# Attention scores in matmuls of 64 rows over six PSUM banks, with the softmax steps in a new order

## The reference

```python
q = split_heads(x @ w_q)
k, v = split_heads(text @ w_k), split_heads(text @ w_v)             # 56 keys
k_ip, v_ip = split_heads(ip_h @ w_k_ip), split_heads(ip_h @ w_v_ip) # 8 keys
out  = merge(softmax(q @ k.T / sqrt(32)) @ v)
out += merge(softmax(q @ k_ip.T / sqrt(32) + mask_ip) @ v_ip)
return out @ w_out + b_out + x
```

## Time and profile before

| | us |
|---|---|
| median of 3 runs | 879.96 (879.78 to 881.93) |
| the profiled execution | 879.29 |
| its span | 877.5 |
| TensorE busy | 872.8 (99%) |
| TensorE weight loads busy | 750.8 (86%) |
| VectorE busy | 724.0 (83%) |
| ScalarE busy | 589.9 (67%) |
| GpSimd busy | 524.2 (60%) |

### The profile page before, as it was taken

The page is one execution under the profiler, slowest core; times in us unless marked ns, Lnnn a source line. Parts: engine busy times, 40 slices in busy tenths (PEclk is TensorE's granted clock), DMA queues, the critical chain, the costliest instruction groups (busy, mean ns, idle before and its releaser), DMA issues.

```text
span 877.5 us, 13695 instructions
## 1 busy us (share of the span) xinstructions
PE 872.8 (99%) x4716; PEld 750.8 (86%) x4716; DVE 724.0 (83%) x1018; ACT 589.9 (67%) x986; POOL 524.2 (60%) x421
## 2 busy tenths in 40 slices
PE   9999999999999999999999999999999999999998
PEld 8899888888888888888888888888888888888877
DVE  7779889797888879697887879787897979888785
ACT  7766685857767585766768486675758577574773
POOL 1059776492846648293755739384664929466581
PEclk9999999999999999999999999999999999999999
DMA  9924223021030303003030301203030210301011
GB/s 324 356 95 135 83 77 127 1 67 70 1 127 1 135 1 116 12 8 128 1 128 1 135 1 41 87 1 135 1 127 1 85 50 1 120 25 37 1 49 72
DMA packets 34225, 64.99 MB, mean 74 GB/s; under 512 B 4480, under 2 KB 6784, under 8 KB 34048
## 3 DMA queue, kind: packets, MB, share of 16 engines
q1 hardware_dynamic: 33888, 62.84, 21.2%
q10 hardware_dynamic: 288, 1.44, 0.4%
HBM read 40.34 MB, written 23.59 MB: 73 GB/s over the span
## 4 chain that ended last, share of the span: by engine, by line
PE 96%; DVE 2%; POOL 1%; ACT 1%; DMA 0%; issue 0%; SPq 0%
PE bank L95 25%; PE bank L97 25%; PE bank L96 25%; PE bank L1155 8%; PE bank L1175 4%; PE bank L1176 4%; PE bank L1064 1%; PE bank L1067 1%; PE bank L1070 1%; DVE total L225 1%; PE bank L1085 1%; PE bank L1082 1%; DMA w_raw<-in_L_xattn_w_k 0%; DVE top L219 0%; POOL prob L178 0%; PE bank L1107 0%
## 5 line engine op out<-in xcount | busy, mean ns | idle before, releaser
L517 POOL TENSOR_TENSOR oT_lo<-o_raw,oT_hi 128x512 fp32r<-128x512 f32 x78 | 100.9, 1294 | 225.0 <-ACT oT_hi L693 225.0
L178 POOL TENSOR_TENSOR prob<-prob,top 128x1120 f32<-128x1120 f32 x126 | 177.5, 1439 | 0.0
L184 POOL TENSOR_TENSOR prob<-prob,inv 128x1120 f32<-128x1120 f32 x126 | 177.2, 1439 | 0.0
L95 PE MATMUL bank<-xT_hi,wq_hi 128*128 128x512 f32 x400 | 163.0, 407 | 0.0
L937 DVE TENSOR_TENSOR o_raw<-bank,pv_part 64x512 f32<-64x512 f32 x160 | 110.2, 689 | 62.4 <-ACT pv_part L689 59.9
L95 PE MATMUL bank<-oT_hi,wo_hi 128*128 128x512 f32 (+1 forms) x405 | 157.4, 389 | 0.0
L96 PE MATMUL bank<-oT_lo,wo_hi 128*128 128x512 f32 (+1 forms) x405 | 156.7, 387 | 0.0
L97 PE MATMUL bank<-oT_hi,wo_lo 128*128 128x512 f32 (+1 forms) x405 | 156.6, 387 | 0.0
L97 PE MATMUL bank<-xT_hi,wq_lo 128*128 128x512 f32 x400 | 156.5, 391 | 0.0
L96 PE MATMUL bank<-xT_lo,wq_hi 128*128 128x512 f32 x400 | 155.8, 389 | 0.0
L689 ACT ACTIVATE pv_part<-bank 64x512 f32<-64x512 f32 x160 | 94.7, 592 | 62.5 <-PE bank L1176 59.9
(11 more groups left out here) (124 smaller groups left out, 1694.3 us busy)
## 6 DMA issues: line engine op xcount, KB each, us to landing
xin<-in_xT SPq DMA_DIRECT2D x16, 1280.0 KB, 6.9
outT<-res SPq DMA_DIRECT2D x79, 256.0 KB, 6.7
w_raw<-in_L_xattn_w_k SPq DMA_DIRECT2D x8, 320.0 KB, 4.9
w_raw<-in_L_xattn_w_k_ip SPq DMA_DIRECT2D x8, 320.0 KB, 5.4
w_raw<-in_L_xattn_w_v_ip SPq DMA_DIRECT2D x8, 320.0 KB, 3.4
w_raw<-in_L_xattn_w_v SPq DMA_DIRECT2D x8, 320.0 KB, 3.3
v_raw<-v_scratch SPq DMA_DIRECT2D x14, 140.0 KB
prob<-in_textT SPq DMA_DIRECT2D x8, 224.0 KB, 4.4
```

Of the source, the lines that this page charges most:

```text
L95: nc.tensor.matmul(dst, a_hi, b_hi, start=first, stop=False)
L178: ins = eng.tensor_tensor(s, s, top[:, t, n, :].unsqueeze(2).broadcast_to([P, HEADS, k1 - k0]), ALU.subtract)
L184: ins = eng.tensor_tensor(s, s, inv[:, t, n, :].unsqueeze(2).broadcast_to([P, HEADS, k1 - k0]), ALU.mult)
L517: nc.gpsimd.tensor_tensor(oT_lo[:, m, :], o_raw[:, m % 2, :], oT_hi[:, m, :].bitcast(F32), ALU.subtract).then_inc(oT_lo_done, 1)
```

## The change

**Scores.** The key parts move into one tensor `k_parts`, in which each half of 64 rows has its own 2 heads x 64 keys = 128 columns. A step becomes six matmuls of 64 rows and 128 columns, the upper and the lower half in turn, each half into a bank of its own (`score_units`). Four steps fill two banks, and the banks rotate over 0 to 5; banks 4 and 5 are those of the value products, so the third pair of banks waits for `pv_added`. The copy now scatters a bank over `prob` (`score_dst`).

```diff
-        def units_for_tile(t):
-            return -(-(t + 1) * SW // 512)
+        def units_for_tile(t):
+            return 2 * -(-(t + 1) * KD // RUN)
...
+        def score_units(pe, g, u, b, new_batch):
+            if u == 0:
+                wait(pe, score_copied, UNITS * g)
+            elif u == 1:
+                wait(pe, pT_lo_done, PAIRS * g)
+            elif u == 2:
+                wait(pe, pv_added, PAIRS * g)
+            else:
+                pe.wait_ge(score_copied, UNITS * g + 2 * u - 4)
...
+            for i in (1, 0, *range(2, RUN)) if u == 1 else range(RUN):
...
+                for n, (q, part) in enumerate(((qT_hi, 0), (qT_hi, 1), (qT_lo, 0))):
+                    for r in range(2):
+                        rows = slice(r * HP, (r + 1) * HP)
+                        ins = nc.tensor.matmul(s_bank[(2 * u + r) % 6][:, i * PW:(i + 1) * PW], q[rows, m, q_cols], k_parts[rows, m, part, :], start=n == 0, stop=n == 2)
```

```diff
         def maxima(dve, g, t):
-            dve.wait_ge(mask_added, GT * g + t + 1)
+            dve.wait_ge(score_copied, UNITS * g + units_for_tile(t))
             for n, (k0, k1) in enumerate(SPANS):
+                if n == 1:
+                    dve.wait_ge(mask_added, GT * g + t + 1)
...
+                    oT_part(g - 1, KD - 1)
+                    for t in range(GT - 1):
+                        maxima(dve, g, t)
+                    split_x(0, 2)
+                    output(g - 1, 1 - u, 0)
+                    maxima(dve, g, GT - 1)
+                    split_x(2, 3)
+                    output(g - 1, 1 - u, 1)
+                    sums(dve, g, 0)
+                    output(g - 1, 1 - u, 2)
+                    split_x(3, 4)
+                    sums(dve, g, 1)
+                    split_x(4, 5)
+                    output(g - 1, 1 - u, 3)
+                    sums(dve, g, 2)
+                    sums(dve, g, 3)
+                    output(g - 1, 1 - u, 4)
+                    if u == 0:
+                        v_lo_part(b)
```

**TensorE at the start of `values`.** The eight transposes of pairs 0 and 1 go tile by tile, both pairs for a tile, where before they went pair by pair:

```diff
-                    p_transpose(g, 0)
-                    p_transpose(g, 1)
+                    pe.wait_ge(score_copied, UNITS * (g + 1))
+                    for t in range(GT):
+                        pe.wait_ge(prob_done, GT * g + t + 1)
+                        for p in range(2):
+                            ins = transpose_tile(g, p, t)
```

```diff
-                sp.dma_start(ctx_raw[:, 0, 0:TT], textT[0:P, :]).then_inc(ctx0_loaded, 16)
                 load_chunk(0)
+                sp.dma_start(ctx_raw[:, 0, 0:TT], textT[0:P, :]).then_inc(ctx0_loaded, 16)
...
+                    if name == "q":
+                        sp.dma_start(xin[:, 0, k, :], x_half[0, 0][:, k, :]).then_inc(first_x_loaded[k], 16)
...
+                nc.gpsimd.memset(v_parts[:].rearrange("p n s c -> p (n s c)").bitcast(F32), 0.0).then_inc(v_zeroed, 1)
+                normalise(pool, 0, 3, 1)
```

More of the change, by code:

```diff
@@ L486, in _ @@
                                         pattern=[[-1, P]], channel_multiplier=1).then_inc(ident_made, 1)
[L487 to L488 removed]
+                nc.gpsimd.memset(k_parts[:].rearrange("p m s c -> p (m s c)").bitcast(F32), 0.0).then_inc(k_zeroed, 1)
                 mine = pool_chunks
@@ L979, in last_softmax @@
                 def last_softmax(g):
-                    for t in range(GT - 1):
+                    oT_part(g - 1, KD - 1)
+                    for t in range(GT):
                         maxima(dve, g, t)
                     sums(dve, g, 0)
-                    maxima(dve, g, GT - 1)
-                    sums(dve, g, 1)
                     dve.wait_ge(max_done, GT * (g + 1))
                     subtract_top(nc.vector, GT - 1).then_inc(last_max_subbed, 1)
-                    for t in range(2, GT):
+                    for t in range(1, GT):
                         sums(dve, g, t)
@@ L1027, in values @@
                                 pT_part(g, p)
+                        if keys is not None and s in (0, 2):
+                            k_lo_part(dve, keys, range(s, s + 2))
                 def group(g, u, b):
                     softmax(g, u, b)
-                    values(g)
-                nc.vector.memset(v_parts[:, :, 1, :].bitcast(F32), 0.0).then_inc(v_lo_zeroed, 1)
+                    values(g, keys=b + 1 if u == 1 else None)
+                v_lo_part(0)
                 q_lo_part(dve, 1, 1)
@@ L1036, in _ @@
                 group(1, 1, 0)
-                with dve.Fori(1, B - 1) as b:
+                for b in range(1, B - 1):
                     group(2 * b, 0, b)
@@ L1137, in _ @@
                         ins.then_inc(k_ipT_ready, 1)
-                for n in range(UNITS):
-                    score_unit(pe, 0, n, 0, True)
+                for u in range(UNITS // 2):
+                    score_units(pe, 0, u, 0, True)
                 for k in range(KC):
@@ L1216, in scores @@
                 def scores(g, b, new_batch):
-                    for n in range(UNITS):
-                        score_unit(pe, g, n, b, new_batch)
+                    for u in range(UNITS // 2):
+                        score_units(pe, g, u, b, new_batch)
                     for m in range(KD):
@@ L1239, in last_group @@
                 def last_group(g, b):
-                    for n in range(UNITS):
-                        score_unit(pe, g, n, b, False)
+                    for u in range(UNITS // 2):
+                        score_units(pe, g, u, b, False)
                     for m in range(KD - 1):
```

164 lines of the change are left out of this document (75 added, 89 removed).

## The result

The changed kernel takes 905.53 us (median of 4 runs, 905.46 to 905.88), the kernel before 879.94 in the same comparison (879.78 to 881.93): ratio 1.0286, 95% interval 1.0268 to 1.0304. The profiled execution took 905.46 us, its span is 903.7 for 877.5. The forecast of 849.6 us is wrong in sign, and the time lies far outside the range of 838 to 877.

What follows compares the result with a forecast made beforehand. TensorE, busy 99% of the span, was taken as the bound. 14 middle groups x (2.6 - 0.6) = 28.0, last group 1.3 and start 0.4 make 29.7 off the profiled 879.3: 849.6 us, range 838 to 877.

Steps and rivals of the forecast that it cites:

- What bounds the kernel now: Whole kernel: TensorE, busy 99% of the span, bounds it until another engine is late.
- the 1.1 us to spare: Softmax stretch: GpSimd ends at 298.09, the fourth tile is needed at 299.19, so the softmax has 1.1 us to spare.
- What the new matmuls cost: Scores: a pair of half matmuls takes 66 ns, side by side with loads hidden, 3.96 us for 60 pairs.
- first rival: Scores: loads decide, halves side by side, 109 to 120 ns a pair; 868 to 878 us, chance 0.25.
- The line through 512, 448 and 320 columns: Matmul price by columns: 0.417 ns a column and 13 ns on top, giving 66 ns for 128 columns.
- What is late in the scores: Third and fifth pairs of banks wait, 0.6 us in all; scores end at +4.6, shrinking by 2.6 us.
- What the softmax then allows: Softmax stretch: VectorE's third inverse delays GpSimd, so TensorE waits 0 to 0.9 us a group, taken as 0.6.
- Key remainders "lie in the values stretch, where VectorE has 5.3 us": Values stretch, odd groups: 4.25 us of moved key remainders are covered; up to 4.25 in 7 groups if not.
- First group: First group: GpSimd is late there, its chain keeps its length and gains a memset; 0, bounds +1 and -1.
- Start: Kernel start: weights issued earlier, at 0.73 for 1.18, bring TensorE's first matmul forward; 0.4 us gained.
- Last group: Last group: the softmax's end decides, and its chain loses the 1.29 us remainder; 1.3 us gained.
- Given back by the other engines: Middle groups: copies, third inverse or key remainders cost 1.3 to 1.7 us more a group; 858 to 868, chance 0.08.
- The case that ended slower: Scores: loads one behind the other, 218 ns a pair, 13.1 us for 7.19; 967 up to 990, chance 0.11.

Runs made afterwards that it cites:

- the halves alone: Kernel before with `k_parts`, `score_units`, six banks and the scattered copy, softmax orders as before: 882.05 us, ratio 1.0025.
- run with 64 columns of weights: Kernel before with 128 columns in each score matmul and only 64 of each 128 tokens as weights, three quarters of the scores left out: 864.96 us.
- one half alone: Changed kernel without the matmuls of the lower half, half the scores left out: 969.37 us.

## Why the prediction was wrong, step by step

**What bounds the kernel now: half right.** TensorE bounds it, and GpSimd's end of the softmax held nobody up in the middle groups. But the 1.1 us to spare were read from an even group. In an odd one VectorE's first query remainder ended 0.06 us ahead of the matmul that needs it, so what TensorE saves there alone is not gained; the halves alone show it.

**What the new matmuls cost: the first step that failed.** The price of 66 ns for a pair is the term. The halves do run side by side, as taken. But the pair costs 0.114 us (6.85 / 60), by the first rival's mechanism. The line through 512, 448 and 320 columns was true for what it was drawn from: with a load of 64 columns a matmul of 128 columns comes every 60 ns. It says nothing of the load, and here the load is longer than the columns. For the load I had two rows, 0.11 us in the same number format and 0.06 us in the same shape, and chose the shape. Both have 128 columns, and the number of rows turned out to decide nothing. What sets the two apart is therefore either the number format or the transposition; no run here took these apart. A row of the kernel before could have told: its transposing loads of 128 rows record 140 ns, as long as those of 64 rows, so the 64 rows were not what made them short. The row that says "loads busy 7.18 of 7.19 us" spoke for the rival in the same text. Size: 0.34 us a group for 2.6, 14 x 2.26 = 31.6 us. The stated point (wrong if the pair is slower than 85 ns) was the right one.

**What is late in the scores: not reached**, since neither wait exists at 0.11. The run with 64 columns of weights, at 0.06 us a matmul and with four banks, does show TensorE waiting for the copies.

**What the softmax then allows: half right.** The first subtraction begins at 227.12 - 221.09 = +6.0, for +5.5 forecast and +7.2 before. GpSimd waits for VectorE's inverses, 1.65 us for the second and 0.22 for the third, where I had expected it at the third:

```profile
239.26 2.94 POOL L185 TENSOR_TENSOR prob<-prob,inv 128x1120 f32<-128x1120 f32 x2
243.85 2.81 POOL L185 TENSOR_TENSOR prob<-prob,inv 128x1120 f32<-128x1120 f32 x2 [1.65 <-DVE inv L243]
246.88 4.94 POOL L185 TENSOR_TENSOR prob<-prob,inv 128x1120 f32<-128x1120 f32 x4 [0.22 <-DVE inv L243]
```

It still ends at 251.82, and TensorE comes to the transposes at 252.78, so the wait I priced at 0.6 us a group does not exist. The one that does is 0.9 us, earlier, at the second query block. Here the step failed by what it left out: I followed VectorE's new order as far as `inv` and asked only who waits for that. The last output tile moved behind two sums in the same list, and who waits for it was never asked. With the stretch at +1.03 for a forecast +0.6, this is 14 x 0.43 = 6.0 us. That GpSimd's own wait stayed away is no sign of room: its end is +30.7 in an odd and +31.2 in an even group, for 29.9 to 30.1 forecast, and TensorE is late by itself. With the last output moved forward again, only 0.26 us are left in even groups from GpSimd's end to the seventh transpose, where the tile is needed.

**Key remainders "lie in the values stretch, where VectorE has 5.3 us": the second large failure.** The 5.3 us are real, but they are a sum over pauses of 0.35 to 1.15 us in a serial exchange between TensorE, ScalarE and VectorE. The bound of "4.25 in 7 groups if the cover failed" was the right kind of number; 2.2 of it came. With the 0.1 us in even groups: 7 x 2.2 + 0.7 = 16.1 us.

**First group: right**, 0. **Start: nothing** for 0.4: the first score begins at 52.04, as before. The two loads changed places, and now the tokens are the second: they are issued at 1.18 us and take 3.18, their rounding begins at 4.38, and TensorE's first product follows at 4.87 for 4.82. I had asked what hangs on the weights and not what hangs on the tokens.

**Last group:** 0.45 us slower for 1.3 faster. I took GpSimd's chain, and TensorE waits for VectorE's multiplication. Counted from the first score it begins at +21.2 for +21.4, so the new order brings 0.2 us there, and it takes 2.92 us for 2.30; TensorE resumes at +24.3 for +23.9. The halves alone make the group 0.95 slower, so the new order takes back half of that. 1.75 us.

31.6 + 6.0 + 16.1 + 0.4 + 1.75 = 55.9 us, from 849.6 to 905.5: nothing is left over.

**The rivals.** "Loads decide, side by side" had the mechanism and the pace, and still gave 868 to 878: it took the softmax as not late. "Given back by the other engines" had the second half of the truth (key remainders, VectorE), but at 858 to 868, on top of a gain that was not there. The result is both together, and no case combined them. The case that ended slower hung on loads in turn, which did not happen.

Three sums of the prediction do not come out as written, and none of them changes what is said above. With waits of 0 and 1.2 us a group the time is 840 to 859, not 838 to 858. A loss of 1.3 to 1.7 us more a group gives 868 to 873; 858 to 868 belongs to 0.6 to 1.3 us. The x remainders ahead of the third inverse are five, as the sum has them, not the four of the list.

What stays open: whether the 0.06 us loads owe it to their format or to the transposition; why the first group of the halves alone is 0.25 us longer; and why its first score begins 0.57 us later. That last one may be chance: the kernels with the same code at the start as the kernel after begin their scores anywhere from 51.96 to 52.97.

## What to carry to other kernels

Price a small matmul by two lines, its moving columns and its weight load, and take the longer, and take the load's price from a row of the same number format and the same operation. Read an engine's room in every kind of group, since the one with the least decides. Free time of an engine is worth what its single pauses hold, so before moving work into a stretch compare the piece with the pause ahead of each consumer, not with the sum. When an order is rewritten, ask for every item that moved later who waits for it, and do not add the gains of two repairs while one wait can hide the other.

## What the runs showed of the hardware

**The clock can fall while only 64 of the 128 rows work.** The kernel with one half alone (one run) has a mean granted clock of 0.915, all others 1.00. Its page (tenths of the clock in 40 slices), and two windows of one group's scores:

```profile
PEclk9979979899898989889797989979798997979899
```

```profile
122.62:126.00 3.38, 3.38 (x31) 3.38 (x31) 1.97 (x4) 2.77 (x6) 1.52 (x1) 1.00 0.04 14
127.00:132.50 5.50, 5.50 (x28) 5.38 (x27) 4.24 (x6) 2.17 (x4) 3.83 (x5) 0.50 0.66 231
```

TensorE issued without a pause, at the pace of the pair; the 64 other rows were idle. Within the scores the grant went from the higher level (2.4 GHz) to the lower (1.2 GHz), and the distance from 0.11 to 0.21 us. It was still the lower one at the start of the softmax stretch, which took 25.9 us for 24.9. With 128 rows and the same 128 columns, or with both halves at work, it stayed full, and so it did with 128 rows and 64 columns of weights. The kernel took 64 us more than the one after (969.37 for 905.53), with half of the score work.

**A border between 128-row and 64-row matmuls costs about 0.1 us** on either side: 0.33 for 0.23 going in, 0.34 for 0.23 coming out, with the load not taken ahead. The Trainium skill (TensorEngine Tiling (Array Packing), Key Properties) says that changing the mode drains the array. The trace does not contradict it, but does not show it as the cause either: in the kernel before, with 128 rows throughout, the first query matmul behind the transposes is followed by the next at 0.31 us for 0.23 (257.01 to 257.32).

**VectorE's x remainders grew** from 1184 to 1386 ns in the mean of all 80 (1204 and 1434 in two groups), the same instructions. They now lie otherwise beside GpSimd's: two took 3.25 us from 230.38, the second of them 2.56 beside a long subtraction of GpSimd's from 230.56, and one 2.40 from 239.48, beside a long multiplication from 239.26. One that lay beside a short subtraction took 0.81 (235.72), and one that began at 243.69, while GpSimd still waited, 0.63.
